# The third scan in units of 1024 columns, u and the decays side by side in two 64-row tiles of the TensorE array

## The reference

```python
chunks = xn.reshape(B, L, 4, dm)...          # 4 groups of channels, L = 1024 tokens
dt = softplus(dtr @ dt_w.T + dt_b)           # per token and channel (di = 32)
A = -exp(A_log)                              # 32 x 16
def step(h, inp):
    dt_t, B_t, C_t, x_t = inp
    dA = exp(dt_t[..., None] * A)
    h = dA * h + (dt_t * x_t)[..., None] * B_t[:, None, :]
    y = einsum('bds,bs->bd', h, C_t)
y = ys + xc * Dp
```

## Time and profile before

| | |
|---|---|
| median of 3 runs | 2015.61 us (2015.4 to 2015.81) |
| the profiled execution's own time | 2014.68 us |
| its span | 2012.7 us |
| busy: PE, DVE, ACT, POOL | 82%, 79%, 58%, 58% |
| mean granted clock | 0.942 |

### The profile page before, as it was taken

How to read it: one execution, slowest core, us unless ns; L and a number is a source line. 1 busy time by engine, 2 the same in 40 slices (tenths; PEclk the granted TensorE clock), 3 DMA queues, 4 the chain that set the end, 5 groups by cost and what they waited for, 6 DMA issues and landing times. The chain is left out here.

```text
span 2012.7 us, 31048 instructions
## 1 busy us (share of the span) xinstructions
PE 1651.0 (82%) x9878; PEld 979.8 (49%) x9878; DVE 1585.5 (79%) x1549; ACT 1158.2 (58%) x1889; POOL 1168.7 (58%) x881
## 2 busy tenths in 40 slices
PE   5888787996788888888888888657888888888787
PEld 2555444884444454444545544234555554554333
DVE  3788745554799999999999999441899999999854
ACT  3444484334666666666666665265666665665356
POOL 0666501001467767676776775202899999999701
PEclk8999988997899999999999999777999999999898
DMA  4000000000254444444444444200000000000001
GB/s 135 2 0 0 1 0 1 1 1 1 53 95 88 90 90 87 94 83 94 89 89 83 94 91 92 44 1 0 1 1 0 0 0 0 0 0 0 7 5 42
DMA packets 23435, 78.21 MB, mean 39 GB/s; under 512 B 3792, under 2 KB 4816, under 8 KB 23120
## 3 DMA queue, kind: packets, MB, share of 16 engines
q0 software_dynamic: 18432, 67.12, 17.6%
q1 hardware_dynamic: 4944, 10.35, 1.8%
HBM read 8.25 MB, written 2.10 MB: 5 GB/s over the span
## 5 line engine op out<-in xcount | busy, mean ns | idle before, releaser
L1173 POOL TENSOR_TENSOR s_prod<-s_ahead,s_cs 128x1024 f32<-128x1024 f32 x128 | 312.2, 2439 | 203.7 <-DVE s_back L1150 103.1
L1708 POOL TENSOR_TENSOR r_prod<-r_state,r_cs 128x512 f32<-128x512 f32 x256 | 322.4, 1298 | 14.8 <-DVE r_state L1649 14.2
L1147 DVE TENSOR_TENSOR_SCAN s_ahead<-s_fore,s_pfeed 128x1024 f32<-128x1024 f32 x128 | 292.7, 2287 | 11.8 <-ACT s_fore L1069 5.3
L1150 DVE TENSOR_TENSOR_SCAN s_back<-s_aft,s_pfeed 128x1024 f32<-128x1024 f32 x128 | 289.5, 2261 | 0.0
L1069 ACT ACTIVATE s_fore<-s_pd,s_aneg 128x896 f32<-128x896 f32 x128 | 129.7, 1013 | 161.0 <-PE s_pd L940 161.0
L940 PE MATMUL s_pu<-s_partsu,selr 128*128 128x512 f32 x512 | 173.4, 462 | 52.2 <-DVE s_pfeed L1140 52.0
L1636 DVE TENSOR_TENSOR r_feed<-r_pu,r_bs 128x512 f32<-128x512 f32 x256 | 164.4, 687 | 61.9 <-PE r_pu L1478 61.9
L1140 DVE TENSOR_TENSOR s_pfeed<-s_pu,s_bs 128x1024 f32<-128x1024 f32 x128 | 157.8, 1233 | 37.7 <-PE s_pu L940 25.0
L1601 ACT ACTIVATE r_decay<-r_pd,r_aneg 128x512 f32<-128x512 f32 x256 | 168.3, 686 | 23.2 <-PE r_pd L1478 23.0
L1478 PE MATMUL r_pu<-r_parts,selr 128*128 128x512 f32 x512 | 161.3, 437 | 5.7 <-DVE r_feed L1636 5.7
L1649 DVE TENSOR_TENSOR_SCAN r_state<-r_decay,r_carry,r_feed 128x512 f32<-128x512 f32 x128 | 156.3, 1263 | 0.0
(11 more groups left out here) (255 smaller groups left out, 3338.1 us busy)
## 6 DMA issues: line engine op xcount, KB each, us to landing
s_ahead<-s_back POOLq DMA_DIRECT2D x128, 512.0 KB, 4.5
x_act<-in_x_dram SPq DMA_DIRECT2D x8, 256.0 KB, 5.4
out_dram<-x_act SPq DMA_DIRECT2D x16, 128.0 KB, 2.3
k_scan<-in_pack_scan_dram SPq DMA_DIRECT2D x1, 1600.0 KB, 10.4
k_fir<-in_pack_fir_dram SPq DMA_DIRECT2D x1, 1600.0 KB, 13.8
k_l<-in_pack_l_dram SPq DMA_DIRECT2D x1, 450.0 KB, 6.9
k_ln<-in_pack_ln_dram SPq DMA_DIRECT2D x3, 131.0 KB, 3.0
k_mlp<-in_pack_mlp_dram SPq DMA_DIRECT2D x2, 194.0 KB, 5.1
```

Of the source, the lines that this page charges most:

```text
L1147: dve.tensor_tensor_scan(ahead[:, v % 4], f, feed[:], 0.0, ALU.mult, ALU.add).then_inc(ahead_done, 1)
L1150: dve.tensor_tensor_scan(back[:, v % 4, ::-1], a[:, ::-1], feed[:, ::-1], 0.0, ALU.mult, ALU.add).then_inc(back_done, 1)
L1173: pool.tensor_tensor(prod[:, b], ahead[:, v % 4], cs[:, buf].rearrange("p i n -> p (i n)"), ALU.mult).then_inc(prod_done, 1)
L1708: pool.tensor_tensor(prod[:, v % 2, q], state[:, v % 2, q], cs[:, v % UNROLL // 4, q], ALU.mult).then_inc(multiplied, 1)
```

## The change

`scan3` is rebuilt around units of 1024 columns: one q and one g of both chunks of a sequence together, so 128 units (`UNITS`), 16 to a sequence and 32 to a turn of the loop. Eight units in a row hold q 0 and 2 in turn (then q 1 and 3), for g 0 to 3. No carry is needed, since a scan of 1024 columns is a whole sequence. `ps_d`, `ps_u` and `feed` are one tile of 1024 columns each (two banks) in place of two tiles of 512.

- PE: u of unit s-16 and delta of unit s-15 are spread with selectors and data of 64 rows (`tile_position` 0 or 64). As units alternate between q 0/1 (rows 0 to 63) and q 2/3 (rows 64 to 127), the two always lie in different halves of the array, and their matmuls are issued in turn: u, delta, u, delta, four of each. Before, each used all 128 rows.
- The rest of B and C: a matmul with `negid` (minus the identity) adds minus the high part to `ps_m`, and ACT copies that out; POOL's subtraction L1713 and the copy `bcf` are gone. `one-1` moves from POOL (`grown`) to ACT. `relu` is written into `delta`.
- y: `place` (fp32, scaled by Dp) writes the skip into `ps_y` by two fp32 matmuls of 512 columns per eight units, ahead of the sums; then for every second unit four 32-column tiles. ACT copies `ps_y` back to `xc` in four pieces of 32 x 512 per eight units, in place of DVE's L1665. POOL multiplies `state` in place, four buffers of it; `prod` is gone.
- Constants: `place` (4 x 128 columns) and `negid` (128) join the pack `l3`.

```diff
-            def spread(bank, sel, which, par):
...
+                k, par, gi = u % 8, u // 16, s - u % 8
+                if k == 2 and live(s, UNITS):
...
+                    pe.wait_ge(hi_bc, gi + 8)
+                    pe.matmul(ps_m[:], negid[:], parts_bc[:, par, 0, at], start=False, stop=True,
+                              skip_group_check=True).then_inc(bc_rest, 8)
+                p, e = s - LAG_D, s - LAG_E
...
+                    if (u - LAG_D) % 16 == 0:
+                        pe.wait_ge(lo_u, p + 16)
+                    wait(pe, fed, p)
...
+                    wait(pe, decayed, e)
...
+                for chunk in range(2):
+                    for part in range(2):
+                        for bank, parts, q, g in jobs:
+                            rows, at = slice(q // 2 * 64, q // 2 * 64 + 64), slice(chunk * N, (chunk + 1) * N)
+                            mm = pe.matmul(bank[:, at], selr[rows, (4 * q + g) * P:(4 * q + g + 1) * P],
+                                           parts[rows, part, at], start=(part == 0), stop=(part == 1),
+                                           tile_position=(q // 2 * 64, 0))
...
+                    wait(pe, s_copied, w)
+                    if k == 1 and live(s, UNITS):
+                        pe.wait_ge(relu_done, gi + 8)
+                    if k == 2 and live(s, UNITS):
+                        pe.wait_ge(lo_bc, gi + 8)
...
+                o, z = s - LAG_Y, (u - LAG_Y) % UNROLL3
+                if z % 2 == 1 and live(o, UNITS):
+                    if z % 8 == 1:
+                        wait(pe, y_done, o - 1)
+                        for chunk in range(2):
+                            pe.matmul(ps_y[:], place[:, 2 * phase + chunk],
...
+                    pe.wait_ge(multiplied, o + 1)
...
+                    mm.then_inc(y_part, 2)
+                if k < 2 and live(s, UNITS):
+                    if live(w, UNITS):
+                        pe.wait_ge(s_copied, w + 1)
+                    if k == 0:
...
+                        pe.matmul(ps_m[:], wdt[:], xc[:, columns(gi, N)], start=True, stop=True).then_inc(dt_ps, 8)
                     else:
+                        pe.wait_ge(relu_done, gi + 8)
+                        pe.matmul(ps_m[:], c["wbc"], xc[:, columns(gi, N)], start=True, stop=True).then_inc(bc_ps, 8)
```

ACT's order in a step is: the four copies of y (k=3), `lo_bc` (k=2), the decay of unit s-15, one copy of B or C for unit s-11, then the front end: |dt|, relu, exp (k=0), `hi_bc` and `one` (k=1), `ln` and `one-1` (k=2), `hi_d` (k=4), `hi_u` (k=5). k is s modulo 8. POOL does the product of unit s-18, then three operations of the softplus (k=3), du (k=4), `lo_d` (k=5), `lo_u` (k=6). DVE:

```diff
+                    dve.wait_ge(u_rep, p + 1)
...
+                    wait(dve, scanned, p)
+                    dve.tensor_tensor(feed[:], ps_u[:], bs[:, phase, q // 2], ALU.mult).then_inc(fed, 1)
+                    dve.wait_ge(fed, p + 1)
+                    dve.wait_ge(decayed, p + 1)
+                    wait(dve, y_part, p - 3)
+                    dve.tensor_tensor_scan(state[:, v % 4], decay[:, v % 4], feed[:], 0.0, ALU.mult,
+                                           ALU.add).then_inc(scanned, 1)
```

More of the change, by code:

```diff
@@ L1435, in scan3 @@
         c, const_in = consts["l3"]
[L1436 to L1451, removed]
+        wdt, place, negid = m.sb("r_wdtb", [P, P]), m.sb("r_place", [P, 4, P]), m.sb("r_negid", [P, P], F32R)
@@ new lines, in scan3 @@
+        delta, du, ex, one, ln = (m.sb("r_" + t, [P, N]) for t in ("delta", "du", "ex", "one", "ln"))
+        parts_d, parts_u, parts_bc = (m.sb("r_parts" + t, [P, 2, 2, 2 * N], F32R) for t in ("d", "u", "bc"))
+        decay, state = (m.sb("r_" + t, [P, 4, 2 * N]) for t in ("decay", "state"))
+        bs, cs = (m.sb("r_" + t, [P, 2, 2, 2 * N]) for t in ("bs", "cs"))
+        ps_d, ps_u, feed = (m.banks("r_p" + t, 1, (P, 2 * N))[0] for t in ("d", "u", "feed"))
+        ps_m, ps_y = (m.banks("r_p" + t, 1)[0] for t in "my")
@@ L1550, in _ @@
+            skewed3(pe, body)
         @block.scalar
@@ L1614, in body @@
[L1614 to L1620 removed]
+                k, par, gi, gm = u % 8, u // 16, s - u % 8, s - u % 16
+                at = slice(u % 16 // 8 * N, (u % 16 // 8 + 1) * N)
+                o, z = s - LAG_V, (u - LAG_V) % UNROLL3
+                if z % 8 == 7 and live(o, UNITS):
+                    phase = z % 16 // 8
+                    act.wait_ge(y_part, o + 1)
+                    for chunk in range(2):
+                        for q in (phase, phase + 2):
+                            rows, src = slice(q * 32, q * 32 + 32), (q ^ chunk) * 32
+                            done = act.activation(xc[rows, columns(o - z % 16 + 8 * chunk, N)], ps_y[src:src + 32],
+                                                  ACT.Copy)
+                    done.then_inc(y_done, 8)
@@ new lines, in body @@
+                if k == 2 and live(s, UNITS):
+                    act.wait_ge(bc_rest, gi + 8)
+                    act.activation(parts_bc[:, par, 1, at], ps_m[:], ACT.Copy).then_inc(lo_bc, 8)
+                e, v = s - LAG_E, u - LAG_E
+                if live(e, UNITS):
+                    g = cells(v)[3]
+                    act.wait_ge(d_ps, e + 1)
+                    wait(act, scanned, e - 3)
+                    act.activation(decay[:, v % 4], ps_d[:], ACT.Exp, scale=aneg[:, g:g + 1]).then_inc(decayed, 1)
@@ new lines, in body @@
+                w = s - LAG_B
+                if live(w, UNITS):
+                    _, phase, _, _ = cells(u - LAG_B)
+                    slot = (u - LAG_B) % 8
+                    which, qi, chunk = slot // 4, slot // 2 % 2, slot % 2
+                    act.wait_ge(s_rep, w + 1)
+                    wait(act, (fed, multiplied)[which], w - slot - 8)
+                    act.activation((bs, cs)[which][:, phase, qi, chunk * N:(chunk + 1) * N], ps_m[:],
+                                   ACT.Copy).then_inc(s_copied, 1)
```

356 lines of the change are left out of this document (145 added, 211 removed).

## The result

| | before | after |
|---|---|---|
| median | 2015.71 us | 2111.3 us (2108.98 to 2111.55, 4 runs) |
| ratio to before, 95% | | 1.0471 (1.0458 to 1.0484) |
| span, mean granted clock | 2012.7 us, 0.942 | 2107.2 us, 0.909 |
| first feed to end of last scan | 491.1 us | 579.2 us |

The account below looks back on a forecast made before the run. POOL (88.5 of 90 us busy) was taken as the bound, DVE 6% behind. Groups of 14 x 32.9 + 2 x 30.2 = 521 against 491.1 gave +30, together with head, tail and preparations +33: 2048 us, range 2001 to 2086.

Parts of the forecast that it names:

- the sum: Third scan: floor 29.3, stalls 3.3 and switches 0.3 us per eight units, plus head and tail; +33 us in all.
- DVE's floor: DVE in the third scan: feed, scan and gap at least 3.66 us a unit, 29.3 per eight against 30.7 before.
- the path: Order of waits among DVE, PE and ACT through one group of eight units; claimed 3.3 us of DVE stalls a group.
- PE's durations on the path: PE matmul times in a group, such as 0.233 us each, 1.06 for y and 1.74 for `place`.
- the clock as a rival: PE's reduced work lowers its clock; at 1.2 GHz a quarter of the time, +2.2 us a group, 2080; chance 0.11.
- feed, k=2: DVE's feed stalls 1.2 us at step k=2, as u queues in PE's list behind `negid`, which waits for `hi_bc`.
- scan, k=2: DVE's scan at step k=2 waits 0.2 us more for the y that frees its state buffer.
- scan, k=4: DVE's scan at step k=4 stalls 1.9 us, because y has `place` ahead of it in PE's list.
- period: Time per eight units in the third scan: 32.9 us in 14 groups, 30.2 in the last two.
- The rival without overlap: The two 64-row tiles do not overlap on PE: u and delta take 0.94 us more each step; 2095 us, chance 0.12.
- Switching the form: Changes of PE's array tiling, two more a unit, add 0.3 us a group; by the skill's drain rule 1.0.
- Head and tail: Third scan's ends: first feed 1.5 us later, ACT's y copies after the last scan add 1.6 us.

Follow-up runs that it names:

- filler: New kernel with four zero-weight matmuls (128 rows, 512 columns) added into `ps_y` at the end of six of eight steps; 2088.14 us, ratio 1.036.
- place_negid: New kernel with the `place` matmuls moved to the end of k=3 and the `negid` matmul behind u and delta of k=2; 2054.28 us, ratio 1.0192.
- full_rows: New kernel with u and delta spread over all 128 rows, without the 64-row tiles; 2113.68 us, ratio 1.0487.
- before_64_rows: Kernel before, its order untouched, with u and delta spread from 64 rows (tile position 0 or 64); 2168.0 us, ratio 1.0754.

## Why the prediction was wrong in size

**Right.** POOL stopped being the bound: the product took 2.37 (2.44 in the sum), POOL is busy 116 of 160 us, 73%, less than the 83% named because the period grew. DVE's floor is 3.66. The decay took 1.11 (1.12), the y copies 2.39 (2.3). The tiles overlap in full. And the path: a feed late behind `negid`, a scan late behind `place`, both shown by moving each.

**The step that failed: PE's durations on the path, taken at the full clock.** The sum took 0.233 a matmul, 1.06 for y and 1.74 for `place`, from stretches at 1.00, and kept the clock as a rival of 0.11 with +2.2 a group. DVE's waits in the 13 groups from 1451.65 to 1934.17 (with front end, without the first):

| | forecast | mean (lowest to highest) |
|---|---|---|
| feed, k=2 | 1.2 | 2.63 (1.56 to 3.44) |
| scan, k=2 | 0.2 | 1.35 (0.56 to 1.91) |
| scan, k=4 | 1.9 | 2.98 (1.46 to 3.92) |
| scan, k=6 | none | 0.75 (0 to 0.97) |
| the rest | none | 0.32 |
| period | 32.9 | 37.1 |

The greater miss is at k=2, 3.98 where 1.4 was forecast, and not behind `place` at k=4, 2.98 where 1.9 was. Five of the 13 groups are nearly the same; one of them, counted from the feed at 1746.17, follows the forecast within 0.1 us up to the start of ACT's `hi_bc` (10.06, forecast 10.05). Then PE's clock is low from `negid` on:

```profile
1756.97 0.76 PE L1507 MATMUL r_pm<-r_partsbc,r_negid 128*128 128x512 f32 x1 [0.83 <-ACT r_partsbc L1640]
...
1759.66 1.22 PE L1549 MATMUL r_pm<-r_partsbc,selr 128*128 128x512 f32 x2
1760.82 1.94 PE L1566 MATMUL r_py<-r_state,ysel 128*32 128x512 f32 x8
```

u starts at 11.49 (forecast 11.0), the feed at 13.60 (12.2), the scan at 16.74 (13.65). In the group counted from 1894.69 PE has the full clock until 1912, and there it is 11.20, 12.43 and 14.23, and PE starts k=4 at 18.88 (18.45). So the path itself was short by 0.2 to 0.6 us, and the rest went with the low clock. The filler's groups at the full clock say the same: of the 4.2 us by which the period is over the forecast, at most 1.3 stay there, and some 3 are the clock's. As a mean of the 13, `place` takes 2.64 to the next start, +0.9 over the 1.74 of the sum; the group shown first, with 3.44, is one of three above 3.3, and one had 1.80.

The rival had the right kind of loss and too small a size: it let PE be slow for a quarter of its time, and it was granted 0.82 to 0.85, which is slow for about a third. It was not spread at random either. In ten of the 13 groups the four pairs of k=2 run at the low level (1.93 to 2.01 us instead of 1.13), behind two waits of 1.3 and 0.8 us for ACT; the idle stretch of k=3 (2.4 to 3.2 us) stands in seven. The rival without overlap gave 2095, for a form that ran at 2113.68, so it was short as well.

**What the clock does not explain.** The four kernels with 128 rows that were granted 0.99 to 1.00 are 46 to 53 us over before, at a floor 23 us under it, and the filler's groups at the full clock are 3.5 us over it each. In place_negid a group takes 33.0, of which 3.7 is stall. The longest in most groups is the scan's at k=2, 1.9 us in all 13 groups whatever the clock; here 1.87 behind a feed's 0.75. PE there, at the full clock:

```profile
1619.27 1.10 PE L1580 MATMUL r_pm<-y_inner,k_l 128*128 x2 [1.32 <-issue]
1620.30 0.50 PE L1522 MATMUL r_pu<-r_partsu,selr 64*128 64x512 f32 x1
...
1621.10 0.39 PE L1522 MATMUL r_pu<-r_partsu,selr 64*128 64x512 f32 x1
...
1621.42 0.50 PE L1531 MATMUL r_pm<-r_partsbc,r_negid 128*128 128x512 f32 x1
1622.77 0.71 PE L1549 MATMUL r_pm<-r_partsbc,selr 128*128 128x512 f32 x2 [0.84 <-ACT r_partsbc L1607]
1623.40 1.06 PE L1567 MATMUL r_py<-r_state,ysel 128*32 128x512 f32 x8
```

`ps_m` is one bank: BC waits for the copy of the spread before it, u of k=2 stands behind BC, the next spread waits for the copy of the rest, and y stands behind that spread. Each round trip between PE and ACT must fit under one scan of 2.29 us, where the second scan had two. In each order that I ran a wait was left in this chain, at one place or another. In the orders with `place` at the end of k=3 it waits for ACT's y copies, 16.6 us between 1500 and 1900 in place_negid, with u of k=4 behind it. That a second bank for the spreads would end it was not tried, and which single link holds the last 40 us stays open.

**Switching the form.** full_rows has the same list without the switch, and so isolates it. Where PE does not wait, at k=2 and the full clock: from `negid` to the first u 0.40 (1905.49 to 1905.89) against 0.30 in full_rows, the spacing behind it 0.34 (to 1906.23) against 0.23, and from the last pair to the spread 0.33 (1906.69 to 1907.02) against 0.23. That is 0.2 for going into the 64-row form and 0.1 for leaving it. Behind y the next u starts 0.99 later with tiles and 1.00 without, and the spacing behind it is 0.34 in both, so a switch from the column tiles cost nothing more. On the path that makes some 0.4 a group; the sum had 0.3. The Trainium skill (TensorEngine Tiling (Array Packing), Key Properties) states that the array drains when the mode changes; the estimate of 1.0 a group that I put beside it is not borne out: the trace shows 0.1 to 0.2 us at a change of the row tiles and none beyond that at the column tiles.

**Head and tail.** +4.1 instead of +1.5; in place_negid the first feed is at 1415.46, +1.4, so the rest went with the two moves or with the clock, which one I didn't separate. Tail +2.6 instead of +1.6. **Unforeseen:** POOL's product waits for ACT's late copy of C, 62.9 us between 1500 and 1900. In the groups read above this delays nothing: every y starts right behind the matmuls ahead of it in PE's list, and PE shows no wait for POOL there.

## What to carry to other kernels

When a change halves the number of units, count how much time one unit of the bounding engine leaves for each round trip through the others: here two alternating 1.2 us scans became one of 2.3 with one buffer of everything, and 5% less time at DVE's pace (29.3 against 30.7) turned into 18% more (36.2). Price a clock rival on the path, not on the average: ask at which steps the granted clock is low and who waits for the matmuls there, and read it in all groups; the group that I read first had its low stretches elsewhere than most. When two cures each gain, run the pair too, and with the suspected resource taken out (here the clock). Ask what else that edit changes: full rows brought the clock back and gave up the overlap, while the filler's groups at the full clock kept both, and what is left there is another cause.

## What the runs showed of the hardware

Matmuls over 64 rows in place of 128 went with a lower granted clock: 0.53 to 0.73 with PE 93 to 97% busy in before_64_rows against 0.91 to 1.00 before, and 0.82 to 0.85 in the new kernel against 0.96 in full_rows with the same order and nearly the same busy share (77 and 80%). Two tiles of 64 rows in different halves run fully at once (pairs 0.233 apart). Going into that form cost 0.2 us and leaving it 0.1 (after against full_rows). At the low level pairs follow at 0.43, eight matmuls of y take 1.94 instead of 1.06, and the four records of two fp32 matmuls take up to 3.4 instead of 1.74. Zero-weight matmuls over 128 rows in PE's gaps went with a higher clock (0.95 to 0.98 against 0.82 to 0.85) and made the kernel 23 us faster; whether the filled gap or the full rows did it was not separated, and in two other orders they gained nothing or cost 6 us.
